# Opening of a two-layer transformer kernel: order of the first loads, batch 0 normalised alone, and products of zeros ahead of the modulation

## The reference

```python
mod = (_silu(L0_c) @ L0_wmod).reshape(L0_c.shape[0], 6, 1, -1)      # 256 x 1536 weights
sa, ca, ga, sb, cb, gb = (mod[:, 0], ..., mod[:, 5])
ga = (2 * (ga >= 0) - 1) * jnp.maximum(jnp.abs(ga), 0.25)           # gb alike
h = _layernorm(x, axis=-1) * (1 + ca) + sa
x = x + ga * _L0_attn_ref(h, L0_attn_w_qkv, L0_attn_w_out)          # sliding window, 16 heads of 16
h = _layernorm(x, axis=-1) * (1 + cb) + sb
x = x + gb * _L0_ffn_ref(h, ...)                                    # 16 experts, top 4, and a shared one
# layer 1: the same with its own weights, causal attention with shared k and v, 8 experts, top 2
```

## Time and profile before

| | |
|---|---|
| median of 3 runs | 636.39 us (634.04 to 637.16) |
| the profiled execution | 634.54 us, span 632.7 us |
| TensorE busy | 591.4 us (93%), 3826 matmuls |
| VectorE busy | 369.5 us (58%) |
| ScalarE busy | 291.6 us (46%) |
| GpSimd busy | 117.8 us (19%) |
| chain that ended last | PE 70%, DVE 19%, ACT 5%, DMA 2% of the span |

### The profile page before, as it was taken

How to read it: one execution, slowest core, us unless ns; L and a number is a source line. 1 busy time by engine, 2 the same in 40 slices (tenths; PEclk the granted TensorE clock), 3 DMA queues, 4 the chain that set the end, 5 groups by cost and what they waited for, 6 DMA issues and landing times.

```text
span 632.7 us, 10398 instructions
## 1 busy us (share of the span) xinstructions
PE 591.4 (93%) x3826; PEld 459.1 (73%) x3826; DVE 369.5 (58%) x725; ACT 291.6 (46%) x450; POOL 117.8 (19%) x90
## 2 busy tenths in 40 slices
PE   4898999998999999999999798889999999999995
PEld 3788645686898888888887465544447788888885
DVE  6477756755444545455557789893476523344456
ACT  3666775564323333333342563348763744333331
POOL 4400031223112222211230000003101331122220
PEclk9998999999999999999999799999999999999999
DMA  8464674000011111111100024402210000111101
GB/s 315 131 223 138 213 222 148 2 10 16 26 51 50 50 36 39 50 50 50 50 26 1 0 74 142 125 31 91 80 37 2 26 25 26 51 50 50 50 1 67
DMA packets 22195, 44.66 MB, mean 71 GB/s; under 512 B 3632, under 2 KB 7632, under 8 KB 22160
## 3 DMA queue, kind: packets, MB, share of 16 engines
q1 hardware_dynamic: 21840, 44.05, 21.9%
q10 hardware_dynamic: 320, 0.13, 0.1%
HBM read 33.16 MB, written 11.01 MB: 70 GB/s over the span
## 4 chain that ended last, share of the span: by engine, by line
PE 70%; DVE 19%; ACT 5%; DMA 2%; issue 2%; POOL 1%; SPq 0%; ACTq 0%; DVEq 0%
PE PS L559 33%; PE PS L1000 16%; DVE nmx L1606 6%; PE PS L883 4%; PE PS L852 2%; PE PS L720 2%; PE PS L718 2%; PE PS L831 2%; PE PS L836 2%; DVE stats L1493 2%; DVE x L1673 1%; DMA qk_slot<-rows_scr 1%; PE PS L898 1%; PE PS L597 1%; DVE xn L1818 1%
## 5 line engine op out<-in xcount | busy, mean ns | idle before, releaser
L1323 ACT ACTIVATE qk_hi<-xn 128x512 fp32r<-128x512 f32 x82 | 51.7, 631 | 166.6 <-DVE xn L1818 137.0
L559 PE MATMUL PS<-h_hi,wqkv_hi 128*128 128x512 f32 x304 | 103.0, 396 | 3.0 <-DVE h_lo L1527 2.2
L559 PE MATMUL PS<-h_hi,wqkv_lo 128*128 128x512 f32 x272 | 92.4, 396 | 1.8 <-DVE xn L1728 1.8
L1815 DVE TENSOR_TENSOR prs<-prs,PS 128x512 f32<-128x512 f32 x60 | 41.2, 687 | 84.7 <-PE PS L559 84.6
L525 POOL TENSOR_TENSOR wqkv_hi<-fw_raw,wqkv_hi 128x768 fp32r<-128x768 f32 x18 | 33.1, 1838 | 244.4 <-ACT wqkv_hi L1299 244.4
L1822 DVE TENSOR_TENSOR qk_lo<-xn,qk_hi 128x512 fp32r<-128x512 f32 x70 | 48.4, 692 | 50.3 <-ACT qk_hi L1323 50.3
L1319 ACT ACTIVATE prs<-PS 128x512 f32<-128x512 f32 x82 | 48.7, 594 | 49.5 <-PE PS L559 49.5
L559 PEld LDWEIGHTS PS<-h_hi,wqkv_hi 128*128 128x128 f32 x304 | 57.2, 188 | 15.3 <-DVE h_lo L1527 2.9
L559 PE MATMUL PS<-h_lo,wqkv_hi 128*128 128x512 f32 x160 | 62.9, 393 | 0.0
L559 PEld LDWEIGHTS PS<-h_hi,wqkv_lo 128*128 128x128 f32 x272 | 51.1, 188 | 13.3 <-DVE xn L1728 2.7
L1000 PE MATMUL PS<-wqkv_hi,qk_hi 128*128 128x256 f32 x280 | 52.1, 285 | 0.9 <-POOL qk_lo L531 0.7
(11 more groups left out here) (266 smaller groups left out, 1176.4 us busy)
## 6 DMA issues: line engine op xcount, KB each, us to landing
fw_raw<-in_ffn SPq DMA_DIRECT2D x41, 384.0 KB, 3.1
qk_slot<-rows_scr SPq DMA_DIRECT2D x32, 200.0 KB
rows_scr<-qk_hi SPq DMA_DIRECT2D x16, 256.0 KB
qk_slot<-q_scr SPq DMA_DIRECT2D x32, 100.0 KB
rows_scr<-qk_lo SPq DMA_DIRECT2D x8, 256.0 KB
wmod<-in_wmod SPq DMA_DIRECT2D x1, 1536.0 KB, 13.1
x<-in_x SPq DMA_DIRECT2D x2, 512.0 KB, 4.3
wmod<-in_wmod SPq DMA_DIRECT2D x1, 1024.0 KB, 9.4
```

The costliest lines, as they stand in the source:

```text
L559: ins = nc.tensor.matmul(dst, left(a, c), right(b, c), start=n == 0, stop=n == total - 1)
L1323: nc.scalar.activation(hidR[b][0], hid[b], ACT.Copy).then_inc(f["hi"], 1)
L1815: tt(hid[buf] if half is None else gu[buf], gact[buf], PS[:, 5, :], ALU.mult).then_inc(f["gu"], 1)
```

## The change

The load of batch 1's rows moves behind `wqkv`. TensorE gets 14 matmuls of zeros of 512 columns into a PSUM bank that is overwritten later, ahead of the modulation's matmuls. VectorE takes the statistics and scales of batch 0 alone and normalises it; batch 1's statistics come after `first_modulation`, its scales after `h_low(0, 0)`. The modulation of batch 0 goes from VectorE to ScalarE. Batch 1's normalisation goes between ScalarE's second and third cast of q and k, its transposes between the projections m = 3 and m = 4, its modulation ahead of `mask_first`, its high part between `mask_first` and `take_v`, and its low part behind the four low parts of q and k.

```diff
             load("ct", ct[:, :, :, :], io["ct"])
-            for b in range(B):
+            def load_x(b):
                 load(f"x{b}", ...)
+            load_x(0)
             load("wmod0a", ...)
             load("ident", ...)
             load("wqkv", ...)
+            load_x(1)
             load("wmod0b", ...)
...
+            pe.wait_ge(consts, 5)
+            for _ in range(14):
+                nc.tensor.matmul(PS[:, 6, :].rearrange("p (r n) -> p r n", n=P), zeroB[:, :],
+                                 zeroB[:, :].unsqueeze(1).to_broadcast([P, S // P, P]), start=True, stop=True)
             pe.wait_ge(sc_done, 1)
...
-            norm_transposes(0)
+            norm_transposes(0, (0,))
...
             for m in range(6):
+                if m == 4:
+                    norm_transposes(0, (1,))
                 project0(0, m)
...  ScalarE
-            norm(0)
+            modulate(0, 0)
+            h_high(0, 0)
...
             for m in range(4):
                 act.wait_ge(proj, m + 1)
                 nc.scalar.activation(qkR[0][:, m, :], PS[:, m, :], ...).then_inc(qhi, 1)
+                if m == 1:
+                    normalise(0)
+            modulate(0, 1)
             mask_first(0, 0)
+            h_high(0, 1)
             take_v(0)
...  VectorE
             spread_silu(0)
-            for b in range(B):
-                dve.wait_ge(loaded[f"x{b}"], 16)
-                statistics(b, range(NT))(b + 1)
-            norm(0)
+            dve.wait_ge(loaded["x0"], 16)
+            statistics(0, range(NT))(1)
+            norm_scales(0, slice(0, 1))
+            normalise(0)
+            dve.wait_ge(wqkv_high, 1)
+            tt(wqkv[1][:, :, :], w_raw[:, :, :], wqkv[0][:, :, :].bitcast(F32), ALU.subtract).then_inc(wqkv_ready, 1)
+            first_modulation()
+            dve.wait_ge(loaded["x1"], 16)
+            statistics(1, range(NT))(2)
+            h_low(0, 0)
+            norm_scales(0, slice(1, B))
...
             for m in range(4):
                 dve.wait_ge(qhi, m + 1)
                 stt(qkR[1][:, m, :], ...).then_inc(qlo, 1)
+            h_low(0, 1)
             maxima_first(0, 0)
```

More of the change, by code:

```diff
@@ L1503, in norm_scales @@
             def norm_scales(n, bs):
-                dve.wait_ge(mv_done, B + 2 * B * (n - 1) + 2 * bs.stop if n else B)
+                dve.wait_ge(mv_done, B + 2 * B * (n - 1) + 2 * bs.stop if n else bs.stop)
                 v, r, w = ve[:, bs, :], rs[:, bs, :], nt_[:, bs, :]
@@ L1528, in h_low @@
                         .then_inc(hl_ready, 1)
[L1530 to L1541, removed]
-                for b in range(B):
-                    h_low(n, b)
             flatT = modT[:, :, :, :].rearrange("p l j b -> p (l j b)")
```

## The result

The changed kernel takes **642.52 us** (median of 4 runs, 641.27 to 647.99) where the kernel before took 636.77 us beside it (4 runs, 634.04 to 639.75). The ratio is 1.0111, interval 1.0067 to 1.0155: slower by about 1.1%. The forecast was 639.3, its range 634.8 to 641.6, so the time lies above the range; the direction, slower, had a chance of 0.41. The profiled execution took 641.27 us (span 639.5) where that of before took 634.54 (span 632.7): 6.7 us more against a forecast of 4.8. Executions at a lower granted clock and over 1.5% above the fastest of their kernel are left out of the ratios and of the medians in the last table.

A forecast was written before the change was run, and what follows sets the result against it. The prediction took an unbroken chain of waits in the opening, from loads to batch 1's projection, as the bound. Its terms, -1.4 + 2.9 + 2.0 + 1.3 = +4.8 us on the profiled 634.54, gave 639.3 us, range 634.8 to 641.6.

The forecast's parts named there:

- parts 1, 2: Opening: earlier weight loads and batch 0 alone on VectorE start batch 0's projection at 16.35 instead of 17.77, -1.4 us.
- part 3: Opening on TensorE: the products of zeros cost 0, bounded by 1.2 us, and are of little use.
- part 5: TensorE's clock: idling makes batch 0's projection start at half clock, +2.0 us, and batch 1's too, +1.3 us.
- part 4: Between the projections: work added to ScalarE's row starts batch 1's 13.05 after batch 0's instead of 10.15, +2.9 us.
- the first term of part 5: Batch 0's projection starts at half clock after 3.6 us of TensorE idle: +2.0 us, bounds 0 and 4.6.
- Rivals 1, 3 and 4: Only first start cold, 638.0 us, chance 0.20; profile's clock throughout, 636.0, 0.13; batch 1's work absorbed, 633.1, 0.11.
- Rival 2: Opening loads: the qkv weights land no earlier, all else as forecast, 640.6 us; chance 0.10.
- Rival 5: Opening on TensorE: the zeros warm nothing, which changes no time; no chance given.

The follow-up runs named there:

- second take: The changed kernel run once more, unaltered, beside the kernel before: 641.56 us (7 runs), ratio 1.0085.
- e1: The changed kernel without its 14 matmuls of zeros and their wait: 641.09 us, ratio 1.0076 to the kernel before.
- e6: The kernel before with only the order of the loads changed: 641.14 us, ratio 1.0077.
- e3: The changed kernel with GpSimd's casts made to wait for the low parts of h: 639.93 us, ratio 1.0054 to the kernel before.
- e8: As e7, with the low part of the qkv weights made by GpSimd instead of VectorE: 638.72 us, ratio 1.000 to the kernel before.
- e2: The changed kernel with more products of zeros (6, 16, 10) filling both TensorE idle stretches: 637.86 us, ratio 1.0012 to the kernel before.
- e4: The changed kernel with batch 1 modulated on VectorE instead of ScalarE: 636.47 us, ratio 1.0004 to the kernel before.
- e7: The kernel before with 18 zero products at the start, 6 ahead of the transposes and 7 behind them: 635.92 us, ratio 0.9996.
- e5: The kernel before with only the 14 products of zeros added: 636.54 us, ratio 0.9997.
- e12: As e11, with 4 products of zeros put back after the first scores: 633.12 us, ratio 0.9954 to the kernel before.
- e9b: The changed kernel with zeros in the idle stretches, GpSimd's waits and batch 1 modulated on VectorE: 634.46 us, ratio 0.9982 to the kernel before.
- e11: As e9b, without the 4 zeros after the first scores and with three masks behind V: 635.09 us, ratio 0.9971 to the kernel before.

## Why the prediction missed

By the steps of its sum, on the profiled executions; the last column is the profile of the second take.

| step | forecast | measured | second take |
|---|---|---|---|
| parts 1, 2: first matmul (17.77) | -1.4 | -0.63 (17.14) | -1.21 |
| part 3: zeros | 0 | none to be told | |
| part 5: batch 0's projection cold | +2.0 | +2.67 (8.35 between starts, against 5.68) | +2.80 |
| part 4: from its end to batch 1's | +2.9 | +2.81 (25.49 to 32.77, against 23.45 to 27.92) | +2.81 |
| part 5: batch 1's start cold | +1.3 | +1.58 (to the last q cast: 9.80, against 8.22) | +1.61 |
| later | 0 | +0.3 | +3.5 |
| sum | +4.8 | +6.7 | +9.5 |

**The mechanism was right in each part**: batch 0's projection starts cold, batch 1's starts late and loses the clock, released by the low part after an idle of over 2 us. What failed is the size of two terms, parts 1 and 2 together and the first term of part 5. Rivals 1, 3 and 4 are out: both cold starts are there (the kernel with a warm TensorE has neither), and the gap grew by 5.5 us. Rival 2 is out as well: the cast of the weights starts at 9.71, not 10.66. Rival 5, that the zeros change no time, holds as far as 5 runs can tell.

**Parts 1 and 2, mis-sized by 0.8 us.** Of it 0.36 is the landing of the weights (9.71 where 9.35 was forecast), which is scatter: the same cast starts at 9.19 in the second take. Another 0.44 is h_low beside GpSimd's cast of the mask. The prediction took 1.29 us from the earlier trace rows, where GpSimd had no cast to make beside it, and did not ask what GpSimd does at the step's new time. (Its 13.0 + 3.27 + 0.06 is 16.33, written as 16.35.)

**Part 4, right.** The second h_low is held by 0.42 too, but V is out only 0.14 us before it, and with GpSimd out of the way V releases the projection at the same distance (7.29 against 7.28). So ScalarE's row cost the 2.8 us, as forecast.

**Part 5, mis-sized by 0.9 us.** I took the mean of two cold stretches of the trace, 3.02 and 6.02 us of cold work. The first cold stretch held 5.86 us of it, nearly the longer. TensorE had stood idle 5.27 us and not the forecast's 3.6: the zeros made the transposes end 0.9 earlier, and the low part came 0.8 later. Five profiles fit this. From the first matmul to batch 1's transposes it is 8.35 and 8.48 us in the two takes, after idles of 5.27 and 4.82 us; it is 7.65, 7.59 and 7.82 in the kernels without the zeros, with GpSimd's waits and with the modulation on VectorE, after idles of 3.85, 3.95 and 3.89. In these three the transposes ran cold (1.86 to 1.97 us), in two of them in spite of the 14 zeros. Against 5.68 that is 1.9 to 2.1 us, the forecast's 2.0. That the longer idle makes the longer cold stretch is what the five suggest; no experiment changed the idle alone. If so, the zeros, priced at 0 in part 3, made the transposes shorter and the cold stretch longer. The upper bound of 4.6 held.

**The base of the sum, a guess that held in part.** The sum was set on the profiled 634.54, 1.85 under the median, on the guess that the median of before already holds about one cold projection. No row of before showed this. The experiments bear on it. For each kernel stands how much later than in the profile of before (36.14) its last cast of batch 1's q starts, behind which the kernels are the same, and how far its median is over before's, timed beside it:

| kernel | opening, us | median, us | difference |
|---|---|---|---|
| after (both takes: +6.43, +6.01; +5.75, +4.66) | +6.2 | +5.2 | 1.0 |
| e1, no zeros | +8.08 | +4.35 | 3.7 |
| e6, load order alone | +7.44 | +4.24 | 3.2 |
| e3, GpSimd waits | +4.51 | +3.19 | 1.3 |
| e8, low part on GpSimd | +4.11 | +1.5 | 2.6 |
| e2, warm | +2.54 | +1.12 | 1.4 |
| e4, modulation on VectorE | +1.96 | -0.27 | 2.2 |
| e7, before, zeros in three places | +1.10 | -0.79 | 1.9 |
| e5, before, zeros in one place | +0.05 | -0.17 | 0.2 |
| e12, masks behind V, zeros | -0.05 | -3.18 | 3.1 |
| e9b, all three | -0.72 | -2.44 | 1.7 |
| e11, masks behind V | -1.15 | -2.9 | 1.8 |

All twelve differences have one sign, and their mean is 2.0 us. What is common to all rows is the profile of before: its opening is shorter than that of a usual execution of the same kernel. By how much is less sure than the mean looks. The profiled executions of the others are on average 0.8 us over their own medians, and a part of this may lie in their openings; and the two latest openings have the largest differences (3.7 and 3.2), so a part may be made up later in the kernel. With that, some 1.2 to 2.0 us are left, about the guessed 1.85. It also bears on why the last version beats before by 3.2 us with an opening that looks no shorter.

Whether these are a cold projection is not shown, since no second execution of before was profiled. For it: the kernel with the load order alone has a cold projection behind the same 16 transposes, which costs it 1.65 us. Against it: zeros ahead of the projection won nothing over before, unless they don't reach far enough.

So the forecast of +2.9 us over the median stands against some +4.9 (641.71 of 11 runs, before 636.8), and the 1.9 us mis-sized in the table of steps, +6.7 for +4.8, are the miss. The rest, up to 642.52, is within what a median of 4 runs scatters. The range was missed by 0.9 us; the second take's median, 641.56, lies just inside it. Its upper end, 641.6, allowed for one dearer cold stretch, and not for the late first matmul beside it. That the second profile is 2.8 us over the first in all, with an opening 0.4 us shorter, says how much of one execution's time is made elsewhere.

## What to carry to other kernels

When a step moves, look up what every other engine does at its new time, GpSimd beside VectorE first, and not only how long the step took at its old time. Work put on an engine whose row ends at the next burst of TensorE can be paid twice, once as idle and once as a burst at half clock; here an idle stretch that stayed was filled with products of zeros, and they paid where they reached up to the burst. A profiled execution 0.3% under the median of its runs can be a base too low by that much, and a second profile of the kernel before would have told where.

## What the runs showed of the hardware

- VectorE's normalisation beside one GpSimd tensor_tensor takes 4.88 us instead of 1.37. Instructions of four elements a partition are held too: the first of batch 1's scales takes 0.63 us at 17.01 beside the mask's cast, and 0.16 where GpSimd waits.
- An idle of 0.93 us left the clock at 1.00, as did 1.85 in the earlier trace rows; 2.64 brought half clock just after the next burst had begun. After 3.85 to 5.27 us the first matmul ran at half clock.
- A short idle is no promise: after transposes that had run at half clock throughout (1.97 and 1.94 us) a burst began at half clock behind 1.09 us of idle.
- Loads land with a scatter of a microsecond: batch 0's statistics start between 4.61 and 6.08 us in the profiled executions, for the same loads ahead of them.
- Executions of the kernel before with the same mean granted clock of 0.990 still differ by 3.8 us (634.31 to 638.07), and a stretch at half clock in the middle of the kernel lasts from 0 to 7 us from one profiled execution to the next. One execution decides nothing under 1% here.
